# A macaron block on one core: the sums of attention moved feature-major by transfers and divided once per eight heads; the norm behind attention in groups of 4 tiles

## The reference

```python
x = L0_attn_x                                      # [1, 4096, 256] f32
x = x + 0.5 * ffn(layernorm(x), ...)               # mixture of 8 experts, see below
x = x + attn(layernorm(x), w_qkv, w_out)
x = x + 0.5 * ffn(layernorm(x), ...)

def attn(x, w_qkv, w_out):                         # 16 heads of 16 features
    q, k, v = split(einsum('bsi,oi->bso', x, w_qkv), 3)       # to heads
    logits = einsum('bhsd,bhtd->bhst', q, k) / 4
    probs = softmax(where(tril, logits, -inf))
    out = einsum('bhst,bhtd->bhsd', probs, v)      # heads side by side: [S, 256]
    return einsum('bsi,oi->bso', out, w_out)

def ffn(x, gate_w, gate_b, w1, b1, w2, b2, w3, b3):
    probs = softmax(x @ gate_w + gate_b, axis=tokens); vals, idx = top_k(probs, 2)
    h = relu(x @ w1[e] + b1[e]); h = relu(h @ w2[e] + b2[e]); y = relu(h @ w3[e] + b3[e])
    v[e] = sum over tokens of y * (the token's weight for e)
    return sum over the token's two experts of v[e]
```

## Time and profile before

| | us |
|---|---|
| median of 3 runs (lowest to highest) | 2117.75 (2114.55 to 2118.36) |
| the profiled execution's own time | 2126.23 |
| its span, first to last instruction | 2124.5 |
| attention's units, first acc to last acc | about 415 to 1794 |
| norm behind attention, last acc to DVE L1475 | 1794.3 to 1855.1 |

### The profile page before, as it was taken

How to read it: one execution, slowest core, us unless ns; L and a number is a source line. 1 busy time by engine, 2 the same in 40 slices (tenths; PEclk the granted TensorE clock), 3 DMA queues, 4 the chain that set the end, 5 groups by cost and what they waited for, 6 DMA issues and landing times.

```text
span 2124.5 us, 99858 instructions
## 1 busy us (share of the span) xinstructions
PE 2047.7 (96%) x43659; PEld 1584.0 (75%) x43659; DVE 1817.7 (86%) x4023; ACT 1598.6 (75%) x3311; POOL 414.5 (20%) x1118
## 2 busy tenths in 40 slices
PE   5899989999999999999999999999999999879998
PEld 3788866377877777777787777777778776658885
DVE  6666666899999999999999999999999994676665
ACT  5344446599999999999999999999999998334442
POOL 1333213411121111121111111111111111023330
PEclk8899989999999999999999999999999999979998
DMA  8211103300010000100001001000010002231112
GB/s 273 74 47 50 42 16 125 134 30 25 13 34 14 25 30 8 34 20 18 31 7 33 22 16 34 9 29 27 11 34 16 22 4 69 54 118 47 45 49 88
DMA packets 70394, 94.36 MB, mean 44 GB/s; under 512 B 16640, under 2 KB 59396, under 8 KB 69956
## 3 DMA queue, kind: packets, MB, share of 16 engines
q1 hardware_dynamic: 62796, 68.75, 10.1%
q0 software_dynamic: 6816, 19.20, 3.4%
q10 hardware_dynamic: 344, 0.01, 0.0%
HBM read 62.24 MB, written 25.43 MB: 41 GB/s over the span
## 4 chain that ended last, share of the span: by engine, by line
PE 88%; DVE 6%; issue 2%; ACT 1%; POOL 1%; DMA 1%; SPq 1%; another core or an unknown queue 0%; DVEq 0%; ACTq 0%; POOLq 0%
PE bank L1264 39%; PE bank L1257 22%; PE bank L1139 17%; PE bank L1346 3%; PE bank L1150 1%; PE bank L1375 1%; DVE stats L1405 1%; PE bank L1307 1%; PE bank L1157 1%; DVE rows L1427 1%; DVE x_res L1725 1%; SPq L698 0%; POOL work L591 0%; DVE work L1594 0%; PE bank L1217 0%
## 5 line engine op out<-in xcount | busy, mean ns | idle before, releaser
L966 ACT ACTIVATE feat<-bank 128x512 f32<-128x512 f32 (+3 forms) x2304 | 1263.2, 565 | 113.8 <-PE bank L1264 13.3
L1264 PE MATMUL bank<-work 96*32 96x512 bf16 (+2 forms) x15872 | 1206.4, 370 | 5.0 <-DVE work L1772 3.8
L1772 DVE TENSOR_REDUCE work<-bank 128x1 f32<-128x512 f32 (+1 forms) x1920 | 1178.9, 659 | 26.4 <-PE bank L1264 23.4
L1257 PE MATMUL bank<-feat,phase 128*17 128x128 f32 (+3 forms) x18432 | 879.2, 263 | 0.3 <-ACT feat L972 0.3
L1257 PEld LDWEIGHTS bank<-feat,phase 128*17 128x17 f32 x18432 | 588.4, 98 | 270.7 <-ACT feat L972 13.7
L1264 PEld LDWEIGHTS bank<-work 96*32 96x32 bf16 (+1 forms) x15872 | 472.6, 96 | 57.1 <-DVE work L1772 24.6
L1139 PE MATMUL bank<-work 128*128 128x256 f32 (+1 forms) x1872 | 398.4, 363 | 0.6 <-issue 0.2
L1139 PEld LDWEIGHTS bank<-work 128*128 128x128 f32 x1872 | 325.1, 192 | 37.1 <-issue 1.0
L625 POOL TENSOR_SCALAR_AFFINE_SELECT feat<-feat 128x128 f32<-128x128 f32 x512 | 145.1, 292 | 456.0 <-ACT feat L966 439.1
L1656 DVE COPY work<-phase 128x514 f32 x234 | 101.5, 436 | 124.1 <-ACT work L880 99.5
L578 POOL DMA_INDIRECT work<-token_table,row_no x142 | 138.1, 973 | 299.0 <-PE bank L1150 142.6
(11 more groups left out here) (201 smaller groups left out, 1371.9 us busy)
## 6 DMA issues: line engine op xcount, KB each, us to landing
phase<-in_w SPq DMA_DIRECT2D x12, 1024.0 KB, 12.0
work<-qk_parts SPq DMA_DIRECT2D x60, 192.0 KB
token_table<-rows SPq DMA_DIRECT2D x8, 1056.0 KB, 8.7
work<-work SPq DMA_DIRECT2D x512, 0.5 KB
qk_parts<-phase SPq DMA_DIRECT2D x20, 384.0 KB, 2.8
work<-qk_parts SPq DMA_DIRECT2D x60, 128.0 KB
qk_parts<-work SPq DMA_DIRECT2D x12, 384.0 KB, 2.8
x_res<-in_x SPq DMA_DIRECT2D x8, 512.0 KB
```

What stands on the lines that cost most here:

```text
L966: eng.activation(p_ring[:, n % P_RING, lo:QB], s_bank("probs", n)[:, lo:QB], ACT.Exp, scale=HD ** -0.5).then_inc(sig.s_done, 1)
L1257: mm = eng.matmul(bank[ACC_BANK][GRID * g:GRID * g + VW, GRID * i0:P], v_aug[:, t, h, :], weights[:, i0:TPJ, g, :], start=(t == 0), stop=( ...
L1264: mm = eng.matmul(out[GRID * g:GRID * (g + 1), width], left[:, GRID * g:GRID * (g + 1)], right, start=start, stop=stop)
L1772: eng.tensor_reduce(maxima[:, h % 2, j, PLACE[i], at:at + 1], scores[:, 0:hi - lo], AX_X, ALU.max).then_inc(sig.a_done, 1)
```

## The change

A unit's sums are no longer transposed and divided one by one. SP moves them by 8 DMAs per unit out of `acc_out` to where they belong with features on the partitions (`heads`, laid over `rows`): 4 DMAs for the sums (16 partitions x 4 runs of 128 bytes), 4 that spread the row of totals over 16 partitions (`totals`; 512 bytes each). When the eighth head of a half is there (h = 7 and 15), 8 items after its `acc`, DVE takes the reciprocal of 128 partitions x 512 totals in place and multiplies 128 x 512 sums: 16 such divisions. `turn`, POOL's multiplication, `transpose_heads` and `copy_heads` are gone, and `acc` waits for the transfers of the unit two before. The norm behind attention works in groups of 4 tiles, with one gate per group; it writes its rows over `work` (`late_rows`) since `rows` holds the heads. The one-hot operands of route(1) move into `rows`. The second experts' loading waits for the last division, their staging for the table's storing.

```diff
-LN_GRP = (4, 4, GRP)
+LN_GRP = (4, 4, 4)
+HEADS_PER_PART = P // HD
+MOVES = 2 * TPJ
-PV_LAG, PV_PAUSE, TURN_LAG, DIVIDE_LAG = 5, 1, 2, 2
+PV_LAG, PV_PAUSE, DIVIDE_LAG = 5, 1, 8
 # attention_steps
-        while unturned and unturned[0][0] <= n:
-            yield "turn", unturned[0][1]
-            undivided.append((n + DIVIDE_LAG, unturned.pop(0)[1]))
                 yield "acc", h * NJ + j
-                unturned.append((n + TURN_LAG, h * NJ + j))
+                if h % HEADS_PER_PART == HEADS_PER_PART - 1:
+                    undivided.append((n + DIVIDE_LAG, h * NJ + j))
 # gpsimd: removed
-                        eng.tensor_tensor(heads[:, TPJ * j:TPJ * (j + 1), h * HD:(h + 1) * HD], sums[:, n % 2, :, 0:HD],
-                                          bc(recip[:, n % 2, :], 2, [P, TPJ, HD]), ALU.mult).then_inc(sig.divided, 1)
 # sync
             def load_experts(f):
                 if f == 1:
                     need.wait_ge(sig.pv, PV_ALL)
+                    need.wait_ge(sig.divided, KD * NJ)
...
+                elif what == "acc":
+                    h, j = UNITS[n]
+                    need.wait_ge(sig.acc, n + 1)
+                    if h >= HEADS_PER_PART:
+                        need.wait_ge(sig.divided, divisions(h - HEADS_PER_PART, j))
+                    at = h % HEADS_PER_PART * HD
+                    for g in range(TPJ):
+                        summed = summed_of(h, j)[at:at + HD, :].rearrange("p (i g b) -> p i g b", i=TPJ, g=TPJ)
+                        eng.dma_start(summed[:, :, g, :],
+                                      acc_out[GRID * g:GRID * g + HD, n % 2, :].rearrange("p (i b) -> p i b", i=TPJ)
+                                      ).then_inc(sig.moved[n % 2], 16)
+                        eng.dma_start(totals_of(h, j)[at:at + HD, g * P:(g + 1) * P],
+                                      bc(acc_out[GRID * g + HD:GRID * g + VW, n % 2, :], 1, [1, HD, P])
+                                      ).then_inc(sig.moved[n % 2], 16)
 # scalar, acc
-                        need.wait_ge(sig.turned, n - 1)
+                        need.wait_ge(sig.moved[n % 2], 16 * MOVES * (n // 2))
 # vector
-                    elif what == "turn":
-                        need.wait_ge(sig.acc, n + 1)
-                        need.wait_ge(sig.divided, n - 1)
-                        eng.transpose(sums[:, n % 2].rearrange("p i w -> p (i w)"),
-                                      acc_out[:, n % 2, :]).then_inc(sig.turned, 1)
                     elif what == "divide":
-                        need.wait_ge(sig.turned, n + 1)
-                        need.wait_ge(sig.divided, n - 1)
-                        eng.reciprocal(recip[:, n % 2, :], sums[:, n % 2, :, HD]).then_inc(sig.recip, 1)
+                        h, j = UNITS[n]
+                        need.wait_ge(sig.moved[n % 2], 16 * MOVES * (n // 2 + 1))
+                        summed = summed_of(h, j).rearrange("p (i g b) -> p i g b", i=TPJ, g=TPJ)
+                        totals = totals_of(h, j).rearrange("p (g i b) -> p i g b", i=TPJ, g=TPJ)
+                        eng.reciprocal(totals_of(h, j), totals_of(h, j)).then_inc(sig.recip, 1)
+                        need.wait_ge(sig.recip, divisions(h, j))
+                        eng.tensor_tensor(summed, summed, totals, ALU.mult).then_inc(sig.divided, 1)
 # tensor, attended: reads heads instead of feat, behind no transpositions
-                        need.wait_ge(sig.heads_copy, KD * (n + 1))
+                    need.wait_ge(sig.divided, divisions(H - 1, i2 // TPJ))
 # stage(f, j, l) on vector
+                if f == 1:
+                    need.wait_ge(sig.table[f], 16 * GROUPS)
```

More of the change, by code:

```diff
@@ L323, in __init__ @@
         self.recip = one("recip")
-        self.pv, self.acc, self.turned = one("pv"), one("acc_copied"), one("acc_turned")
-        self.heads_tr, self.heads_copy = one("heads_tr"), one("heads_copied")
+        self.pv, self.acc, self.moved = one("pv"), one("acc_copied"), many("sums_moved", 2)
         self.out_mm, self.attended = one("out_mm"), one("x_attended")
@@ L426, in macaron_block, with hcarve @@
         hat = [0]
-        def hcarve(n):
+        def hcarve(f, n):
             hat[0] += n * HOTS // 2
[L430 to L434, removed]
+            space = rows[:, :, :].rearrange("p i r -> p (i r)") if f else work
+            return space[:, hat[0] - n * HOTS // 2:hat[0]].bitcast(BF16).rearrange("p (n i) -> p n i", i=HOTS)
+        lo_wide, hi_wide, hot_lo, hot_hi = [], [], [], []
+        for f in range(2):
+            hat[0] = 0
+            lo_wide.append(hcarve(f, P))
+            hi_wide.append(hcarve(f, N_SUB))
+            hot_lo.append([hcarve(f, P) for _ in range(TOP * NT // HOTS)])
+            hot_hi.append([hcarve(f, N_SUB) for _ in range(TOP * NT // HOTS)])
         def bf(ap):
@@ L453, in macaron_block @@
         at_v = NT * H * VW
+        totals = [phase[:, at_v + j * QB:at_v + (j + 1) * QB] for j in range(NJ - 1)] + [spare[:, QB:2 * QB]]
         part_rows = [bf(phase[:, at_v + i * 3 * QB // 2:at_v + (i + 1) * 3 * QB // 2]) for i in range(3)]
@@ L460, in macaron_block, with rows_of, summed_of, totals_of @@
         split_f += [stack[:, 1, 0, S - 2 * QB:S].bitcast(F32)]
-        heads = rows[:, :, 0:D]
+        heads = rows[:, :, :].rearrange("p i r -> p (i r)")[:, 0:KD * S].rearrange("p (k s) -> p k s", k=KD)
+        late_rows = work[:, 0:NT * ROW].rearrange("p (i r) -> p i r", i=NT)
+        def rows_of(f):
+            return late_rows if f else rows
+        def summed_of(h, j):
+            return heads[:, h // HEADS_PER_PART, j * QB:(j + 1) * QB]
+        def totals_of(h, j):
+            return totals[j] if h // HEADS_PER_PART else heads[:, 1, j * QB:(j + 1) * QB]
+        def divisions(h, j):
+            return h // HEADS_PER_PART * NJ + j + 1
         def bc(ap, axis, shape):
@@ L658, in store_table @@
                     eng.dma_start(table[f][1:S + 1, :].rearrange("(i p) r -> p i r", p=P)[:, g * GRP:(g + 1) * GRP, :],
-                                  rows[:, g * GRP:(g + 1) * GRP, :]).then_inc(sig.table[f], 16)
+                                  rows_of(f)[:, g * GRP:(g + 1) * GRP, :]).then_inc(sig.table[f], 16)
             def store_parts(n):
@@ L995, in _ @@
             attention()
-            layer_norm(2, attended, nothing)
+            layer_norm(2, nothing, nothing)
             route(1)
@@ L1510, in route @@
                 prev()
-                step("weights", eng.tensor_tensor(rows[:, :, D:ROW], chosen_bf[:, :, :], probs[:, :, :], ALU.mult))
+                step("weights", eng.tensor_tensor(rows_of(f)[:, :, D:ROW], chosen_bf[:, :, :], probs[:, :, :], ALU.mult))
                 flat_run = scratch[:, 1].rearrange("p i e -> p (i e)")
@@ L1733, in attended @@
             def attended(g):
-                for i2 in range(g * GRP, (g + 1) * GRP, 2):
+                for i2 in range(g * LN_GRP[2], (g + 1) * LN_GRP[2], 2):
                     need.wait_ge(sig.out_mm, KD * (i2 + 2))
```

99 lines of the change are left out of this document (27 added, 72 removed).

## The result

The changed kernel takes 2322.1 us (median of 4, 2316.8 to 2325.5), the kernel before on the same chip 2118.1. The ratio is **1.0965, 95% interval 1.0952 to 1.0978**: 204 us slower. The forecast was 2165 us, with a range up to 2196. The direction was right, the size four times too small, and the result lies outside the range.

A forecast was written before the change was run, and what follows sets the result against it. PE was taken to bound the kernel, with DVE 1.7% behind in attention. Pauses 35.5, clock 11, transfers 3 and norm -2 summed to +47.5 us on the median 2117.75: 2165 us, likeliest case 2140 to 2195, 8 in 10 2116 to 2196.

The forecast's parts named there:

- PE is the bound, DVE close behind: In attention, PE is busy 86.97 of a head's 87 us and DVE 85.52, so long DVE work pauses PE.
- Relief of DVE and POOL worth 0: In attention, removing 58 us of DVE's transpositions and reciprocals and POOL's multiplication gains nothing, as PE hides it.
- The other end, -12: In attention, if PE's 7.1 us of waits per 800 us were real pauses, removing them would gain 12 us.
- Reciprocal 3.2 us: On DVE in each division, a 128x512 reciprocal takes 3.2 us, range 0.72 to 6.7.
- Pauses +35.5, clock +11: In h = 7 and 15, 13 divisions each pause PE 2.7 us; half of 13 x 1.7 us more in clock.
- the 2.4 us: In attention, the time from PE ending a block to wanting the fourth block on: 2.4 us before DVE's lateness pauses it.
- The transfers: +3: On SP's list, new DMAs take 0.42 us each to issue, 3.4 a unit; 3 us in all, ends 0 and 15.
- the signs I named: In the trace: 3.2 us reciprocal, 2 to 3 us pauses, issue rows near 0.37, other heads 86.7 to 87 us.
- The rival "SP is late": On SP's list, 0.66 us per DMA makes divisions wait and ACT miss `acc`; 2212 us, chance 0.09.
- 39 us for divisions waiting: In h = 7 and 15, if SP is late, 13 divisions cost 3 us each by waiting for transfers.
- The norm, -2: Behind attention, from the last sums to route, PE sets turns of 6.0 us; -2 us, ends -8 and +3.
- The rest, 0: After attention, second experts' loading, staging's wait and one-hot operands cost nothing; 1 us if the table is late by that.

The follow-up runs named there:

- 1.4 us of products: The kernel before plus two 128x512 products on DVE at each of the 16 division places, no reciprocal; ratio 1.0079, 1.1 us per division.
- two transfers and narrow divisions: The changed kernel with divisions of 8 columns instead of 512 and 2 transfers per unit instead of 8; ratio 0.9973 to the kernel before.
- Measured alone: The kernel before plus 16 reciprocals and products of 128x512 on a scratch tile, without transfers; ratio 1.0325, 69 us, by the heads 65.4.
- the runs with four and six transfers: The changed kernel with divisions of 8 columns and 4 or 6 transfers per unit instead of 8; ratios 1.0004 and 1.0160 to the kernel before.
- the longer lag: The changed kernel with its divisions 24 items behind `acc` instead of 8; ratio 1.0824 to the kernel before, about 30 us faster than the changed kernel.

## Why the prediction was wrong, point by point

- **PE is the bound, DVE close behind: right.** It explains why nearly every pause is lost: 1.4 us of products cost 1.1.
- **Relief of DVE and POOL worth 0: right.** With two transfers and narrow divisions, 58 us of DVE's small work gone, ordinary heads are at 86.7 to 86.8 against 86.7. The other end, -12, did not come.
- **Reciprocal 3.2 us: right, 3.35.** From 128x8 at 0.202 the slope is 3.15/504 = 6.25 ns per element, where 6.0 was read off two small shapes. The Trainium skill ("VectorE: DVE Perf Modes", First, the fixed hardware budget) states a repeat count of 8 for the iterative divide, by which my estimate from that page was 4.3 us. The trace doesn't agree with reading that as 8 cycles per element: it shows 6.25 ns, where that reading makes 8.3.
- **Pauses +35.5, clock +11: mechanism right, both too small** (13 x 2.7 is 35.1; the slip changes nothing). Measured alone: 65 to 69 us, a pause of 3.2 and a clock loss of 1.7 per division, not half of it. What they give together, 4.9, is the 5.0 measured. Of the 0.5 us that the pause is longer, 0.14 is the division itself (4.07 us for 3.93); the rest is a lead shorter than the 2.4 us that I granted anew to each division, which is argued and was not varied. In the changed kernel itself the wide division was worth only 51, 6.6 of them behind attention (57.3 against 50.7); the likely reason, not tested, is that part of it lies beside waits for SP.
- **"The transfers: +3": this is the step that failed.** It cost 159 us between two and eight transfers. Three of its premises fell. (1) 0.42 us per issue: the shortest rows were 0.61 and 0.59, the mean 0.7. I had taken the 0.31 of some loads in the earlier trace rows for moves of another shape; the 0.61 of `max_row`, in the same rows, was the right neighbour. Of the signs I named, rows near 0.37 did not come, nor did 86.7 to 87 us in the other heads. (2) The 55 of 87 us for SP's load per head are an average; the list overflows at the head's start, where 43 DMAs are due in 23 us and some 31 get out. At the assumed 3.4 us per unit the cost would lie between the runs with four and six transfers (2.6 and 3.9 us), 0.1 to 1.3 us a head, so with (1) right the term would have been small. (3) "`max_row` has a lead of 44 tiles": the scores do. The row of maxima was ready 11.4 us before PE wanted it, SP came to it 9.1 us late, and it landed 5.19 us after its issue, which I had nowhere. I named this DMA and did not price it. What made it land so late is open.
- **The rival "SP is late" (0.09)** had the 0.66 per issue, and 2212, still 110 too low. It charged half a us per head for `acc` and missed `max_row`, whose late arrival, with the clock behind it, is most of the 8 us that an ordinary head lost. Its 39 us for divisions waiting were near the mark (30 by the longer lag).
- **The norm, -2: right in size, in part by luck.** The trace has -3.5. That is the sum of -4.9 (groups of 4), -8.8 (two transfers and a narrow division for the transpositions), +3.5 (eight transfers) and +6.6 (wide division). The forecast's own way there was off twice, in opposite directions: the last division ended 0.9 us later than said, and a turn of PE takes 5.3 us (its projections start at 2011.5, 2016.7, 2022.0 and so on), not 6.0.
- **The rest, 0: right**; it is 265.2 us, and 265.2 to 265.5 in six of the other kernels.

The Trainium skill ("DMA: Bandwidth & Descriptors", Issuing engines are not separate DMA queues) says that the time a sequencer takes to initiate a DMA is usually small relative to the DMA itself. Here it was not: 0.61 to 0.7 us of issue against 2.3 us to landing, and on SP's list the issue times add up, 57 of them to 41.6 us.

## What to carry to other kernels

Price every added DMA at the issue time of its nearest row. Take the stretch in which most of them fall due, add up all that the list must issue in it, old and new, and compare the sum with the stretch's length, not with an average over the whole; then go through everything that stands behind it on the same list and ask how long before its use it is ready. In this kernel an engine within 2% of the bound lost nearly the whole length of an extra piece of work (1.1 of 1.4 us), and a pause of 3.2 us cost another 1.7 in clock. Moves that are not urgent were cheapest in few large DMAs, with their consumers far enough behind that an in-order engine did not stand for them.

## What the runs showed of the hardware that was not expected

- A DMA of [4, 16] rows of 128 B between SBUF tiles, and one that spreads a row over 16 partitions, hold SP for the same 0.61 and 0.59 us at least, with single ones of 1.9 and 2.3 us while many are in flight.
- A `max_row` DMA of 0.5 KB landed 5.19 us after its issue while SP's list was full, and 1.59 us after it where SP had issued nothing for 7 us; the moves of 8 KB landed at a median of 2.3.
- The clock fell to 1.2 GHz behind pauses of PE of 3.2 us (for 3.41 us) and of 4.9 us (for 6.83). With 1.4 us of extra work per division it stayed at 1.00.
- The reciprocal of 128x512 costs 3.35 us on each of three tiles and 3.34 in the kernel before; that of 128x32 costs 0.35.
